# Rope in the turned layout: query, key and latent-key projections with stationary weights, and one wide matmul for the values of a pair

## The reference, cut to what matters

```
q  = x @ w_q            # 32 heads of 128
k  = x @ w_k            #  8 heads
v  = x @ w_v            #  8 heads
lk = (x @ w_lq) @ w_lk  # 32 heads, through 128 latent columns
lv = x @ w_lv           # 32 heads
q, k, lk = rope(q), rope(k), rope(lk)   # y*cos + rotate_half(y)*sin over the head's 128 columns
attn = causal_softmax(q k^T / sqrt(128)) v
lat  = causal_softmax(q lk^T / sqrt(128)) lv
x = layernorm(x + attn @ w_o + lat @ w_lo)
x = layernorm(x + top-1 mixture of 8 rank-16 experts)
```

## Time and profile before

| what | value |
|---|---|
| time, median of 3 runs | 2185.76 us (2184.28 to 2186.39) |
| time of the profiled execution | 2185.91 us |
| its span, first to last instruction | 2184.1 us |
| PE busy | 2102.7 us, 96% of the span |
| DVE busy | 1404.9 us, 64% |
| ACT busy | 1040.6 us, 48% |
| POOL busy | 886.7 us, 41% |
| mean granted clock of TensorE | 0.992 |

### The profile page before, as it was taken

How to read it: one execution, slowest core, us unless ns; L and a number is a source line. 1 busy time by engine, 2 the same in 40 slices (tenths; PEclk the granted TensorE clock), 3 DMA queues, 4 the chain that set the end, 5 groups by cost and what they waited for, 6 DMA issues and landing times.

```text
span 2184.1 us, 44663 instructions
## 1 busy us (share of the span) xinstructions
PE 2102.7 (96%) x14928; PEld 1951.9 (89%) x14928; DVE 1404.9 (64%) x3734; ACT 1040.6 (48%) x2501; POOL 886.7 (41%) x769
## 2 busy tenths in 40 slices
PE   6999999999999999999999999999999999999995
PEld 6989999898998989999899998989999898998983
DVE  4656757576575656757567575666756577575765
ACT  2544626355263643726346263553626446263551
POOL 3434434344353434435344353444434344353430
PEclk9999999999999999999999999999999999999997
DMA  4010010100001010010100001010010000100001
GB/s 154 1 32 11 2 53 1 42 1 34 20 1 42 2 42 11 2 42 1 53 1 11 32 2 52 2 32 11 1 53 2 32 11 20 34 1 30 1 11 39
DMA packets 15511, 50.60 MB, mean 23 GB/s; under 512 B 1696, under 2 KB 3744, under 8 KB 15136
## 3 DMA queue, kind: packets, MB, share of 16 engines
q1 hardware_dynamic: 15264, 47.47, 6.4%
HBM read 45.37 MB, written 2.10 MB: 22 GB/s over the span
## 4 chain that ended last, share of the span: by engine, by line
PE 44%; issue 33%; POOL 19%; DVE 2%; POOLq 1%; ACT 0%; DVEq 0%; ACTq 0%
POOL probs L630 13%; PE ps L270 13%; PE ps L271 12%; PE ps L272 12%; PE ps L358 5%; POOL probs L625 4%; POOL pt_lo L611 2%; PE ps L332 1%; DVE pt_lo L637 1%; DVE stats L781 0%; ACT pt_hi L475 0%; PE ps L453 0%; POOLq L629 0%; PE ps L468 0%; POOL wlk_lo L617 0%
## 5 line engine op out<-in xcount | busy, mean ns | idle before, releaser
L630 POOL TENSOR_TENSOR probs<-probs,inv_sum 128x640 f32<-128x640 f32 (+7 forms) x512 | 586.6, 1147 | 691.7 <-DVE inv_sum L724 690.9
L637 DVE TENSOR_TENSOR pt_lo<-ps,pt_hi 128x512 fp32r<-128x512 f32 (+3 forms) x768 | 401.6, 551 | 185.9 <-ACT pt_hi L475 182.7
L507 ACT ACTIVATE probs<-probs,neg_max 128x640 f32<-128x640 f32 (+7 forms) x512 | 397.6, 777 | 165.3 <-DVE neg_max L717 165.3
L475 ACT ACTIVATE pt_hi<-ps 128x512 fp32r<-128x512 f32 (+3 forms) x768 | 347.0, 486 | 168.7 <-PE ps L358 155.2
L717 DVE CUSTOM_DVE_ANT_0 probs<-ps,mask 128x640 f32<-128x640 f32 (+7 forms) x512 | 383.8, 752 | 59.7 <-PE ps L272 43.1
L270 PE MATMUL ps<-pt_hi,x_hi 128*128 128x256 f32 x1280 | 377.7, 295 | 9.4 <-POOL wlk_lo L617 9.4
L272 PE MATMUL ps<-pt_hi,x_lo 128*128 128x256 f32 x1280 | 363.4, 284 | 0.0
L271 PE MATMUL ps<-pt_lo,x_hi 128*128 128x256 f32 x1280 | 362.8, 283 | 0.0
L358 PE MATMUL ps<-ident,probs 128*128 128x128 f32 x2304 | 336.7, 274 | 9.6 <-POOL probs L630 8.0
L358 PEld LDWEIGHTS ps<-ident,probs 128*128 128x128 f32 x2304 | 267.2, 140 | 41.0 <-DVE pt_lo L637 19.6
L270 PEld LDWEIGHTS ps<-pt_hi,x_hi 128*128 128x128 f32 x1280 | 245.7, 192 | 12.3 <-POOL wlk_lo L617 9.8
(11 more groups left out here) (110 smaller groups left out, 4654.2 us busy)
## 6 DMA issues: line engine op xcount, KB each, us to landing
raw<-wo SPq DMA_DIRECT2D x32, 512.0 KB, 3.3
raw<-wq SPq DMA_DIRECT2D x16, 512.0 KB, 3.3
raw<-wlv SPq DMA_DIRECT2D x16, 512.0 KB, 4.1
raw<-wkv SPq DMA_DIRECT2D x8, 512.0 KB, 3.5
acc<-xT SPq DMA_DIRECT2D x4, 512.0 KB, 5.9
acc<-x SPq DMA_DIRECT2D x1, 2048.0 KB, 7.8
wlk_raw<-wlk SPq DMA_DIRECT2D x16, 128.0 KB, 3.1
out<-acc SPq DMA_DIRECT2D x8, 256.0 KB, 2.4
```

The costliest lines, as they stand in the source:

```text
L475: return nc.scalar.activation(dst, src, ACT.Copy)
L507: nc.scalar.activation(dst, dst, ACT.Exp, bias=neg_max[:, n % 4:n % 4 + 1], scale=-1.0, accum_out=row_sum[:, n % 4:n % 4 + 1]).then_inc(q[ ...
L630: nc.gpsimd.tensor_tensor(b, b, inv_sum[:, k % 4:k % 4 + 1].to_broadcast([P, w]), ALU.mult).then_inc(q["normed"], 1)
L637: return nc.vector.tensor_tensor(dst, src, h, ALU.subtract)
```

## The change

Queries, keys and latent keys are made already turned: the weights of one head (128 columns) are the stationary operand, and 512 tokens move, so a unit is (head, half of the tokens) and its 12 matmuls are 512 wide (3 for a latent key). Rope then works with the head's columns on partitions: cos and sin tables in that layout are made once, at the start (four DMAs instead of two, each into pieces of 64 elements; 16 transposes; six DVE instructions), and the two sin products of `rope` are computed on 64 partitions each, with input and output on opposite halves. The transposes, and with them the copy out of PSUM, go away: POOL adds, ACT rounds the sum in SBUF to the high part (`rope_hi`), and POOL, no longer DVE, subtracts for the low part. The values of a pair (v and the two lv in pair 0, the two lv in pair 1) are one unit for each token tile, 12 matmuls of 384 or 256 columns. The probabilities of two neighbouring tiles share one of three slots of 1152 columns. The first scores are put before the last unit but one (tiles 0 and 1) and before the last unit (tile 2).

```diff
-P_BUFS = 4
+P_SLOTS = 3
+P_COLS = 1152
-POOL_LO = ("q0", "kv", "lv0", "q1", "lv1")
+POOL_LO = ("q0", "k", "v", "lv0", "q1", "lv1")
 UNITS = (
-    [x for t in range(ST) for x in (("ql", t), ("kv", t))] + [("lv", x) for x in range(ST // 2)],
-    [("ql", t) for t in range(ST)] + [("lv", x) for x in range(ST // 2)],
+    [("q", 0, 0), ("q", 0, 1), ("k", 0, 0), ("k", 0, 1), ("lk", 0, 0), ("v", 0), ("lk", 0, 1), ("v", 1), ("q", 1, 0), ("v", 2),
+     ("q", 1, 1), ("v", 3), ("lk", 1, 0), ("v", 4), ("lk", 1, 1), ("v", 5), ("v", 6), ("v", 7)],
+    [("q", 0, 0), ("q", 0, 1), ("lk", 0, 0), ("v", 0), ("lk", 0, 1), ("v", 1), ("q", 1, 0), ("v", 2),
+     ("q", 1, 1), ("v", 3), ("lk", 1, 0), ("v", 4), ("lk", 1, 1), ("v", 5), ("v", 6), ("v", 7)],
 )
+HI_LAG = 3
+def hi_at(pair, u):
+    return [r for r in range(ROPES[pair]) if ROPE_UNITS[pair][r] + HI_LAG == u]
+def wait_probs_free(eng, g, pair, n):
+    before = n - 4 - n % 2
+    if before >= 2:
+        eng.wait_ge(q["turned"], per_pair(g, pair, T_UNITS, UNITS_BEFORE[before]))
+    else:
+        eng.wait_ge(q["rope_lo"], rope_base(g, pair, ROPES[pair] - P_SLOTS + n // 2 + 1))
...
@@ SP, start @@
-            sp.dma_start(cos_sb[:], cos).then_inc(q["tab_in"], 16)
-            sp.dma_start(sin_sb[:], sin).then_inc(q["tab_in"], 16)
+            for slot, table in ((1, cos), (2, sin)):
+                twice = probs[:, slot, 0:2 * ST * HALF].rearrange("p (t f d) -> p t f d", t=ST, f=2)
+                for f in range(2):
+                    sp.dma_start(twice[:, :, f, :], table).then_inc(q["tab_in"], 16)
...
@@ PE, unit(g, pair, u) @@
+                if kind == "v":
...
+                    n0 = HD if pair else 0
+                    for c in range(CT):
+                        mm = three(ps[:, bank, n0:3 * HD], x_tile(c, x), [w[:, c, n0:3 * HD] for w in vals_w], c == 0, c == CT - 1)
...
+                if kind == "lk":
+                    mm = three(ps[:, bank, :], [w[:, HD * x:HD * x + HD] for w in (wlk_hi, wlk_lo)],
+                               [w[:, 512 * h:512 * h + 512] for w in (lq_hi, lq_lo)], True, True)
+                else:
                     for c in range(CT):
+                        mm = three(ps[:, bank, :], [w[:, c, HD * x:HD * x + HD] for w in (q_w if kind == "q" else k_w)],
+                                   [w[:, c, 512 * h:512 * h + 512] for w in (x_hi, x_lo)], c == 0, c == CT - 1)
-            def turn_roped(g, pair, r):
...
@@ ACT, projection stage @@
                     for u in range(len(UNITS[pair])):
-                        if u == len(UNITS[pair]) - 1:
+                        if u == len(UNITS[pair]) - 2:
                             for n in range(EARLY):
                                 exponentials(g, pair, n)
+                        for r in hi_at(pair, u):
+                            rope_hi(g, pair, r)
+                        if UNITS[pair][u][0] == "v":
+                            t, v0 = UNITS[pair][u][1], pair
+                            act.wait_ge(q["val_mm"], per_pair(g, pair, ST, t + 1))
+                            hi(val_hi[:, v0:3, t, :], ps[:, 4 + u % BANKS, HD * v0:3 * HD].rearrange("p (a d) -> p a d", d=HD)
+                               ).then_inc(q["val_hi_made"], 1)
...
@@ POOL @@
+                    for r in range(ROPES[pair] + 1):
+                        if r < ROPES[pair]:
+                            b = probs[:, slot_of_rope(pair, r), :]
+                            pool.wait_ge(q["rope_mul"], rope_base(g, pair, r + 1))
+                            nc.gpsimd.tensor_tensor(b[:, 0:512], b[:, 0:512], b[:, 512:1024], ALU.add).then_inc(q["rope_add"], 1)
+                        if r >= 1:
+                            pool.wait_ge(q["rope_hi"], rope_base(g, pair, r))
+                            h, l = roped(pair, r - 1)
+                            nc.gpsimd.tensor_tensor(l, probs[:, slot_of_rope(pair, r - 1), 0:512], h, ALU.subtract
+                                                    ).then_inc(q["rope_lo"], 1)
                     for k in range(TILES):
...
@@ DVE, rope(g, pair, r) @@
+                dve.wait_ge(q["rope_mm"], rope_base(g, pair, r + 1))
+                if r >= P_SLOTS:
+                    dve.wait_ge(q["rope_lo"], rope_base(g, pair, r - P_SLOTS + 1))
+                nc.vector.tensor_tensor(b[:, 0:512], src, cos_t[:, cols], ALU.mult)
+                nc.vector.tensor_tensor(b[0:HALF, 512:1024], src[HALF:P], sin_t[HALF:P, cols], ALU.mult)
+                nc.vector.tensor_tensor(b[HALF:P, 512:1024], src[0:HALF], sin_t[0:HALF, cols], ALU.mult
+                                        ).then_inc(q["rope_mul"], 1)
...
@@ DVE, projection stage @@
+                    last = len(UNITS[pair]) - 1
+                    for u in range(last + 1):
+                        if u >= 1 and UNITS[pair][u - 1][0] == "v":
+                            values_lo(g, pair, u - 1)
+                        if UNITS[pair][u][0] != "v":
+                            rope(g, pair, ROPE_UNITS[pair].index(u))
+                        if u == last - 1:
                             for n in range(EARLY):
                                 row_max(g, pair, n)
+                        if u == last:
                             for n in range(EARLY):
                                 inverse(g, pair, n)
                             for n in range(EARLY, EARLY + MID):
                                 row_max(g, pair, n)
+                    values_lo(g, pair, last)
```

More of the change, by code:

```diff
@@ L68 @@
 UNITS = (
-    [x for t in range(ST) for x in (("ql", t), ("kv", t))] + [("lv", x) for x in range(ST // 2)],
-    [("ql", t) for t in range(ST)] + [("lv", x) for x in range(ST // 2)],
-)
-ROPES = tuple(sum(k != "lv" for k, _ in u) for u in UNITS)
[4 rows of a table added]
+)
+ROPE_UNITS = tuple([u for u, x in enumerate(units) if x[0] != "v"] for units in UNITS)
+ROPES = tuple(len(x) for x in ROPE_UNITS)
 LN_TILES = ST // 2
@@ L112, with ropes_until, slot_of_rope @@
 SLOTS = max(O_SLOT) + 1
-def turned_at(pair, u):
-    last = ROPES[pair] + R_LAG - 2
-    return (u - R_LAG, u - R_LAG + 1) if u == last else (u - R_LAG,) if R_LAG <= u < last else ()
+HI_LAG = 3
+def hi_at(pair, u):
+    return [r for r in range(ROPES[pair]) if ROPE_UNITS[pair][r] + HI_LAG == u]
+def ropes_until(pair, kind, a):
+    return max(r for r, u in enumerate(ROPE_UNITS[pair]) if UNITS[pair][u][:2] == (kind, a)) + 1
+def slot_of_rope(pair, r):
+    return (r - ROPES[pair]) % P_SLOTS
 def part_of_pt(n):
@@ L215, in raw_of, with roped, probs_of @@
             return raw[:, LOADS.index(name) % RAW_SLOTS, :]
+        def roped(pair, r):
+            kind, a, h = UNITS[pair][ROPE_UNITS[pair][r]]
+            return [(k if kind == "k" else ql[:, a if kind == "q" else 2 + a, :])[:, 512 * h:512 * h + 512]
+                    for k, ql in ((k_hi, ql_hi), (k_lo, ql_lo))]
+        def probs_of(n):
+            w, slot = P * (ORDER[n % ST] + 1), n // 2 % P_SLOTS
+            return probs[:, slot, P_COLS - w:P_COLS] if n % 2 else probs[:, slot, 0:w]
+        def wait_probs_free(eng, g, pair, n):
[4 more added lines that the diff above has]
+                eng.wait_ge(q["rope_lo"], rope_base(g, pair, ROPES[pair] - P_SLOTS + n // 2 + 1))
         def scores_of(n):
@@ L322, in turn_roped, with tables @@
-            def turn_roped(g, pair, r):
-                pe.wait_ge(q["rope_add"], rope_base(g, pair, r + 1))
-                if r == 0:
-                    pe.wait_ge(q["out_added"], SEED + per_pair(g, pair, ST, 0))
-                else:
-                    if r >= 2:
-                        pe.wait_ge(q["rope_lo"], rope_base(g, pair, r - 1))
-                n = 4 if UNITS[pair][r][0] == "ql" else 1
-                for b in range(n):
-                    mm = pe.transpose(ps[:, r % 2, P * b:P * b + P], probs[:, r % P_BUFS, P * b:P * b + P], ident[:])
-                mm.then_inc(q["rope_t"], 1)
+            def tables():
+                pe.wait_ge(q["tab_in"], 64)
+                for y in range(4):
+                    for x in range(4):
+                        mm = pe.transpose(ps[:, y, P * x:P * x + P], probs[:, 1 + y // 2, 512 * (y % 2) + P * x:512 * (y % 2) + P * x + P],
+                                          ident[:])
+                    mm.then_inc(q["tab_turned"], 1)
@@ L338, in scores @@
                 if n == 0:
-                    pe.wait_ge(q["rope_lo"], rope_base(g, pair, ROPES[pair]))
+                    pe.wait_ge(q["out_added"], SEED + per_pair(g, pair, ST, 0))
+                if n % ST == 0:
+                    made = max(ropes_until(pair, "q", a), ropes_until(pair, "lk", a) if latent else 0,
+                               ropes_until(0, "k", 0) if pair == 0 and not latent else 0)
+                    pe.wait_ge(q["rope_lo"], rope_base(g, pair, made))
                 keys = (ql_hi[:, 2 + a, :], ql_lo[:, 2 + a, :]) if latent else (k_hi[:], k_lo[:])
@@ L406, in _ @@
             latent_query()
+            pe.wait_ge(q["const_made"], 2)
+            tables()
```

(10 more changed lines are left out.)

220 lines of the change are left out of this document (85 added, 135 removed).

## The result

The median went from 2186.07 to 2122.86 us (four runs each, 2121.75 to 2125.99 after). The ratio is 0.9714, with a 95% interval of 0.9698 to 0.9731. The prediction was 2115.5 with a range of 2100 to 2138: the time lies inside it, 7.4 us above the forecast. The profiled execution took 2122.39 us, its span 2120.6.

What follows compares the result with a forecast made beforehand. PE was taken as the bound, busy 2102.7 of 2184.1 us. From 2185.9 us, 81.4 came off for PE's stream, 8 was added for pair 1's entry and 3 for the start: 2115.5 us, range 2100 to 2138.

Steps and rivals of the forecast that it cites:

- PE's stream: Projection on PE: transposes removed save 63.2 us, fewer and wider matmuls 18.2, so the instruction stream gets 81.4 us shorter.
- The rope on DVE: Projection: three 512-element multiplies take 1.8 us a rope, 1.9 with the tail, or 2.05 if each is held.
- The entry of pair 1: Projection to attention: PE's first probability transposes wait 1.4 us for POOL, costing 1.0 us each pair 1, 8 us.
- ACT's exponentials end at about 3.9, as before: Entry of pair 1: ACT finishes its exponentials 3.9 us after the first score, ahead of value copy and rope copy.
- Part of it is given back: Entry of pair 1: tile 2's old 0.49 us wait is then covered, so the 1.4 us lateness shrinks.
- The bank wait of q(1,0): Pair 1's projection, second head's second-placed q unit waiting for lk(0,0)'s bank: costed at nothing, at most 0.3 us a pair.
- a sign of being wrong: Bank waits of PE in the projection, POOL operations over 1.4 us, or a start beyond 40 would show the prediction wrong.
- The end of pair 0: Last step of pair 0's attention: attention and output keep their instructions, so any change there was costed at nothing.
- The entry of pair 0: Projection to attention in pair 0: PE wants the transposes at 7.3 us and has them at 7.4; no loss.
- The start: Before PE's first projection matmul: the tables' small DMA pieces delay the load of x, costing 3 us.

Runs made afterwards that it cites:

- order2: Pair 1's units reordered, a latent-key unit behind the first two query units, against the kernel with pair 1's query units first (2110.76 us): 2106.78 us, ratio 0.964.
- POOL twice: One more 512-column subtraction on POOL for each rope, result not used, against the changed kernel: 2236.02 us, ratio 1.0237 to the kernel before.

## Why the prediction came out as it did

- **PE's stream: right.** Transposes gone, 512-wide 0.227 apart, a value unit of pair 0 2.10 us (2.09 expected), of pair 1 1.43. Pair 0 gained 5.53 us; with the 0.37 of the late maximum 5.90, against 5.93.
- **The rope on DVE: under-priced.** This is the term that was mis-sized first. The forecast took 1.9 us, it is 2.13. The rows show 0.71 from start to start, and 0.61 in the kernel in which the first sine product starts where the cosine product does. By the rule in the Trainium skill that the prediction weighed ("VectorE: DVE Perf Modes", section on two Vector instructions with no wait between them), all three multiplies are held: the trace agrees, and the price, 0.11 us for each instruction, is a little over the 0.68 - 0.59 that I bounded it with.
- **The entry of pair 1: mechanism and place right, size wrong.** Predicted 1.0 us a pair. The first value matmul of the attention is at 14.07 us from the first score, 12.37 before: 1.7. The step that failed is "ACT's exponentials end at about 3.9, as before": they end at 4.4 (441.82 + 0.18 - 437.59), since DVE is late with the first maximum. That is 0.4 of the missing 0.7: the transposes are at 7.82 and not at 7.4. The other 0.3 is "Part of it is given back", 0.4 in the forecast: tile 2's wait of 0.49 went, but the first product now waits 0.91 instead of 0.55. 0.7 x 8 = 5.6 us.
- **The bank wait of q(1,0): costed at nothing, 0.36 us.** The forecast had PE at 9.7 and DVE at 9.8 with the slow rope; that was the true case, and with the 2.13-us rope DVE is done at 9.9 (422.70 + 2.1 - 414.93). 2.9 us in all, a little over the bound of 0.3 us a pair. The prediction named such waits as a sign of being wrong, and they came. The kernel with two multiplies shows that it goes with a shorter rope, "order2" that it goes with another order of units.
- **The end of pair 0: missed.** 0.37 x 8 = 3.0 us, from a DVE instruction that starts late with nothing to wait for. Its cause stays open.
- **The entry of pair 0: right.** Its first transposes are at 7.50 us, predicted 7.4, and the pair's difference shows no loss there.
- **The start: wrong sign.** +3 predicted, -0.7 measured. I took half of the full rate, 174 GB/s, and let the rest delay x; the queue moved 225 to 256 GB/s in the gap, and x was issued 0.15 us later than before. I also kept PE's old wait for the wlk split, which no longer stands ahead of the first matmul: the first unit has no latent part now. By the Trainium skill's 27% for small descriptors ("DMA: Bandwidth & Descriptors", on why small descriptors are slow) the term was, as an estimate, about 1: nearer. What the runs show is nothing, within 0.2 us behind the issue of x.

The misses, 5.6 + 2.9 + 3.0 - 3.7 = 7.8 us, stand against the 6.9 between 2115.5 and the profiled 2122.4. The difference between the two was not followed further. The bank wait and about 0.4 of the 0.7 us at the entry come from one fault, a rope on DVE that is longer than priced. That the total came within 7 us is in part luck: the start erred by 3.7 us the other way.

## What to carry to other kernels

Taking instructions out of the bounding engine's stream pays what their spacing in the trace says. What it gives away lies at the seams, where another engine's last piece of work of the old stage stands in order ahead of the first of the new: after such a change, move that last piece forward and put it ahead of the new stage's work on each engine it passes; here this was worth 13 us, and 16, a quarter of the change's own gain, with the order that also frees the banks in time. Before such a change is priced, walk the chain with the slow durations too, since a wait met by 0.5 us on paper is one to expect.

## What the runs showed of the hardware that was not expected

- On DVE an instruction of 512 elements that starts on another partition half than its predecessor follows 0.68 to 0.72 us after it, else 0.59 to 0.61; whether it covers 64 or 128 partitions made no difference.
- A 256-wide fp32r matmul costs 0.1195 us, a 384-wide one 0.174 and a 512-wide one 0.2267. Three 128-wide and three 256-wide ones in turn take 0.68 us, where three 256-wide ones alone take 0.36. An lk unit of three 512-wide ones between 256-wide units takes 0.70 instead of 0.68.
- DVE started one maximum 0.37 us late in every group, at one place of its program, and did not when instructions ahead of it were fewer (two multiplies a rope) or more (24 increments a pair). The cause is open.
- 24 semaphore increments on DVE ahead of the first rope made it start some 2.2 us later at the head of the loop over the groups, and not at all in the middle of its body, where DVE waits 2.03 us for PE in any case.
- After pauses of some 4 us PE worked for 3 to 4 us at a granted clock of 0.50 (1.2 GHz), in all eight groups of "POOL twice"; in four of them the clock had fallen during the pause, some 2 us in.
- POOL's fp32 operations on 128x512 last 1.30 us by the records and can follow one another every 1.25.
